# Moving work across the entrance to the second attention of a gated cross-attention and mixture-of-experts kernel

## The reference

```
x = x + tanh(g_xattn[0]) * L0_xattn(layernorm(x), ctx)    # projections, stablemax attention
x = x + tanh(g_ffn[0])   * L0_ffn(layernorm(x))           # 64 experts, top 8, capacity 128, and a shared expert
x = x + tanh(g_xattn[1]) * L1_xattn(layernorm(x), ctx)    # softmax(q k^T) v per head, q = layernorm(x), k = v = ctx
x = x + tanh(g_ffn[1])   * L1_ffn(layernorm(x))           # 256->1024, butterfly, gelu, butterfly, 1024->256
```

## Time and profile before

| | |
|---|---|
| median of 3 runs | 1233.26 us (1229.75 to 1236.8) |
| profiled execution, own time | 1231.84 us |
| its span | 1229.6 us |
| PE busy | 1034.0 us, 84% |
| DVE busy | 817.2 us, 66% |
| ACT busy | 702.2 us, 57% |
| POOL busy | 360.6 us, 29% |
| mean granted TensorE clock | 0.927 |

### The profile page before, as it was taken

One profiled execution on the slowest core, in us unless ns is written; L12 is line 12 of the kernel. 1 busy time (PEld: TensorE's weight loads), 2 busy tenths in 40 slices (PEclk: granted clock), 3 DMA queues, 4 the chain that ended last, 5 costly groups with the idle time before them and its releaser, 6 DMA issues.

```text
span 1229.6 us, 17473 instructions
## 1 busy us (share of the span) xinstructions
PE 1034.0 (84%) x5635; PEld 751.7 (61%) x5635; DVE 817.2 (66%) x2051; ACT 702.2 (57%) x1351; POOL 360.6 (29%) x313
## 2 busy tenths in 40 slices
PE   4688888888876688998899976888898989899888
PEld 2354544544444577887687755657676767767567
DVE  4468778777778766755667658687567577664543
ACT  1899878988975433565554421364455455544542
POOL 2000000000000003778777631124334251423223
PEclk9779988988887888999999996899999999999998
DMA  6564435434121323788988644331312133120000
GB/s 145 122 153 137 129 95 167 120 82 129 52 73 69 128 61 104 184 203 199 245 198 184 146 119 92 88 109 26 106 46 80 37 104 82 50 56 1 20 18 18
DMA packets 97401, 128.41 MB, mean 104 GB/s; under 512 B 26976, under 2 KB 69344, under 8 KB 97056
## 3 DMA queue, kind: packets, MB, share of 16 engines
q1 hardware_dynamic: 82448, 105.73, 30.0%
q0 software_dynamic: 12288, 18.88, 8.5%
q10 hardware_dynamic: 2576, 2.69, 1.0%
HBM read 66.15 MB, written 30.70 MB: 79 GB/s over the span
## 4 chain that ended last, share of the span: by engine, by line
PE 51%; DVE 26%; ACT 9%; issue 6%; POOL 3%; DMA 2%; SPq 2%; ACTq 2%; DVEq 0%; POOLq 0%
PE psum L912 6%; PE psum L1098 6%; PE psum L1083 5%; PE psum L1001 4%; PE psum L928 4%; PE psum L819 3%; DVE stats L1363 3%; PE psum L795 3%; PE psum L865 3%; PE psum L1030 2%; DVE weights L1484 2%; DVE peaks L1764 2%; PE psum L960 2%; PE psum L741 2%; DVE normed L1404 2%
## 5 line engine op out<-in xcount | busy, mean ns | idle before, releaser
L1863 POOL TENSOR_SCALAR vareps<-moments 128x4 f32<-128x4 f32 x32 | 10.4, 326 | 529.2 <-DVE moments L1366 529.2
L795 PE MATMUL psum<-q_stack,k_stack 96*128 96x512 f32 (+1 forms) x256 | 123.2, 511 | 39.2 <-DVE weights L1484 24.8
L1297 ACT ACTIVATE weights<-psum 128x512 f32<-128x512 f32 x160 | 94.1, 597 | 71.7 <-PE psum L795 60.7
L1484 DVE SCALAR_TENSOR_TENSOR weights<-psum,weights 128x512 f32<-128x512 f32 x160 | 102.5, 681 | 43.2 <-ACT weights L1162 43.0
L1883 POOL DMA_INDIRECT expert_sums<-made,sum_rows x64 | 105.4, 1647 | 59.3 <-DVE made L1734 38.6
L1910 POOL TENSOR_TENSOR hidden<-hidden_whole,hidden 128x512 fp32r<-128x512 f32 x64 | 82.3, 1287 | 114.2 <-DVE hidden L1812 114.2
L1030 PE MATMUL psum<-k_stack,q_stack 96*128 96x256 f32 x256 | 88.2, 395 | 31.9 <-DVE peaks L1764 20.0
L1764 DVE TENSOR_REDUCE peaks<-psum 128x2 f32<-128x308 f32 x256 | 107.0, 469 | 12.1 <-PE psum L1032 11.6
L912 PE MATMUL psum<-feat_parts,w_shared_up 128*128 128x512 f32 x384 | 100.5, 412 | 10.7 <-DVE shared_silu L1608 6.3
L1098 PE MATMUL psum<-w_con_high,hidden 128*128 128x256 f32 x512 | 102.2, 298 | 0.1
L1812 DVE CAST hidden<-hidden_whole 128x512 fp32r<-128x512 f32 x64 | 52.7, 823 | 71.6 <-ACT hidden_whole L1326 70.3
(11 more groups left out here) (211 smaller groups left out, 2390.9 us busy)
## 6 DMA issues: line engine op xcount, KB each, us to landing
expert_w<-in_expert_w SPq DMA_DIRECT2D x64, 384.0 KB
q_stack<-q_stage SPq DMA_DIRECT2D x96, 128.0 KB, 3.0
q_stack<-q_stage SPq DMA_DIRECT2D x174, 64.0 KB, 2.0
expert_sums<-zeros SPq DMA_DIRECT2D x6, 1408.0 KB, 8.2
fetched<-expert_sums SPq DMA_DIRECT2D x16, 512.0 KB, 4.8
rows_scratch<-rows SPq DMA_DIRECT2D x8, 640.0 KB, 3.4
k_raw<-in_k SPq DMA_DIRECT2D x16, 300.0 KB
x<-in_x SPq DMA_DIRECT2D x8, 512.0 KB, 4.8
```

The source lines that it names most:

```text
L795: T.matmul(to, k[0:row, head_at(head), :], q[0:row, head // 2, :], start=True, stop=True).then_inc(scored, 1)
L1297: A.activation(weights1[n % 6][:, :], score_bank[n % 2], ACT.Exp).then_inc(exped, 1)
L1484: V.scalar_tensor_tensor(weights[n % 9][:, :], score_bank[n % 5], 1.0, weights[n % 9][:, :], ALU.add, ALU.max).then_inc(weighted, 1)
```

## The change

- SP no longer fetches half 0 with `fetch(0)` behind the barrier. When all scatters have landed, and before SP waits for the other engines, `fetch_first` loads half 0 of both sums as four DMAs of two tiles each, and the first two parts of the keys follow. They signal on four semaphores of `x_in` that served the first load of x.
- DVE adds half 0 in four instructions of 512 elements instead of two of 1024, and takes the statistics of two tiles behind each pair.
- POOL's `add_experts(1, ...)` waits for the four `key_split1` of DVE instead of the norm of half 0.
- The statistics, norm, `turn_q1` and all sends of half 1 move from between the maxima of half 0 to behind `peaks(0)`, around the first `sh_down`; the second `sh_down` moves from chunk 0 to in front of `scores1(0)`. All 24 sends of half 1 are SP's (six were ACT's).
- Four units of maxima of half 1 move from in front of the loop into it, the others up to two chunks later, and `peaks(1)` from chunk 10 to chunk 12.

```diff
-PEAKS_SECOND = (-1, -1, -1, -1, 1, 2, 3, 4, 5, 6, 7, 7, 8, 8, 9, 9)
+PEAKS_SECOND = (1, 2, 2, 3, 4, 4, 5, 6, 6, 7, 8, 8, 9, 10, 10, 11)
...
 def plan_last():
-    plan = [("fetch", 0), ("load_k1", 0, 0), ("load_k1", 0, 1)]
+    plan = []
...
-    beside_peaks = {4: norm_units("q1", 1)[:2], 7: norm_units("q1", 1)[2:],
-                    9: [("turn_q1", 1), ("send_q1", 1, 0), ("send_q1_a", 1, 1)]}
     for n in range(HT * PAIRS // 2):
         plan.append(("peak", 0, n % HT, n // HT))
-        plan += beside_peaks.pop(n, [])
         if n in LATE_AT:
             late.step()
-    plan.append(("peaks", 0))
-    plan += [("send_q1", 1, two) for two in range(2, PAIRS // 2)]
+    plan += [("peaks", 0)] + norm_units("q1", 1)
     late.step()
-    plan += peak_units(1, -1)
+    plan += [("turn_q1", 1)] + [("send_q1", 1, two) for two in range(PAIRS // 2)]
+    late.step()
     plan.append(("scores1", 0))
...
+        first_sums = x_in[0:2 * SUMS]
...
+            def tile_stats(n, h, t):
+                V.bn_stats(stats[n % 2][:, t, :], x[:, HT * h + t, :]).then_inc(ln_bn, 1)
+
             def norm_stats(kind, h):
                 n = norm_no[kind, h]
-                for t in range(HT):
-                    V.bn_stats(stats[n % 2][:, t, :], x[:, HT * h + t, :]).then_inc(ln_bn, 1)
+                if (kind, h) != ("q1", 0):
+                    for t in range(HT):
+                        tile_stats(n, h, t)
...
-                    else:
-                        V.wait_ge(x_first, SUMS)
...
-            def add_experts(h, i):
+            def add_experts(h, a):
                 if h == 0:
-                    V.wait_ge(fetched_in[i], 16)
-                    if i:
-                        V.wait_ge(x_first, i)
-                    V.tensor_tensor(half_of(0), half_of(0), fetched[i][:, :, :], ALU.add).then_inc(x_first, 1)
+                    tiles = slice(2 * a, 2 * a + 2)
+                    for i in range(SUMS):
+                        V.wait_ge(first_sums[SUMS * a + i], 32)
+                        if i:
+                            V.wait_ge(x_first, SUMS * a + i)
+                        V.tensor_tensor(x[:, tiles, :], x[:, tiles, :], fetched[i][:, tiles, :],
+                                        ALU.add).then_inc(x_first, 1)
+                    V.wait_ge(x_first, SUMS * (a + 1))
+                    for t in range(2 * a, 2 * a + 2):
+                        tile_stats(norm_no["q1", 0], 0, t)
...
                     elif h == 1:
-                        G.wait_ge(ln_normed, HT * (norm_no["q1", 0] + 1))
+                        G.wait_ge(keys_split, BATCH + 4)
...
+            def fetch_first():
+                for i in range(SUMS):
+                    S.wait_ge(scattered[i], 16 * (EXPERTS // SUMS))
+                for a in range(2):
+                    for i in range(SUMS):
+                        S.dma_start(fetched[i][:, 2 * a:2 * a + 2, :], sum_dram[i][2 * P * a:2 * P * (a + 1), :].rearrange(
+                            "(t p) f -> p t f", p=P)).then_inc(first_sums[SUMS * a + i], 16)
...
                 if h == 1:
-                    S.wait_ge(x_first, SUMS)
+                    S.wait_ge(x_first, 2 * SUMS)
...
                     S.drain().then_inc(stage_over, 1)
+                    if n == 2:
+                        fetch_first()
+                        load_k1(0, 0)
+                        load_k1(0, 1)
                     S.wait_ge(stage_over, 5 * n)
```

More of the change, by code:

```diff
@@ L1892, in add_experts @@
                 if h:
-                    G.wait_ge(fetched_in[i], 16 * (h + 1))
+                    G.wait_ge(fetched_in[i], 16 * h)
                     if h >= HALVES - LATE:
@@ L2026, in send_lists @@
                                 list_dram[g].rearrange("(a e) b -> e a b", a=NA)).then_inc(list_in, 16)
+            def fetch_first():
[5 more added lines that the diff above has]
+                            "(t p) f -> p t f", p=P)).then_inc(first_sums[SUMS * a + i], 16)
             def fetch(h):
                 if h == 1:
-                    S.wait_ge(x_first, SUMS)
-                elif h:
+                    S.wait_ge(x_first, 2 * SUMS)
+                else:
                     S.wait_ge(x_added, SUMS * (h - 1))
```

## The result

| | before | after |
|---|---|---|
| median of 20 runs each, compared with each other | 1231.76 us (1227.45 to 1240.68) | 1238.91 us (1231.24 to 1246.35) |
| profiled execution, own time | 1231.84 us | 1232.08 us |
| its span | 1229.6 us | 1230.3 us |
| mean granted clock, profiled execution | 0.927 | 0.929 |
| first PE work behind the barrier to the end of the span | 507.7 us | 513.4 us |

The ratio is 1.0053, with a 95% interval of 1.003 to 1.0076: the change costs about 6.5 us. The forecast was 1234.4 us.

The account below looks back on a forecast made before the run. PE paces the kernel, but half 0 hangs on how early SP sends half 2; earlier gains end in SP's 24 sends and POOL's addition, moving that send from 805.74 to 806.8, +1.1 us on 1233.26: 1234.4 us, range 1227.5 to 1239.5.

Parts of the forecast that it names:

- the upper bound of the sum: First send of half 2: at worst +5.0 us, against the forecast's +1.1.
- no gain from the first sums: Start of half 0: upper-bound case in which the early loads come no earlier, +2.3 us.
- late keys: Last key loads before the maxima of half 0: upper-bound case with keys at 739.7, +0.8 us.
- transposes at half clock: Chunk 12, before the sends of half 2: upper-bound case of slow transposes, +0.8 us.
- The steps up to the loop: Barrier to scores1(0): shorter sums and maxima, first send of half 1 at 768.4, scores1(0) 5.6 us ahead.
- The step that failed: Chunk 10: the loop, about 5.5 us ahead, leaves DVE waiting about 2 us for POOL's sum at 793.4.
- The maxima's move into the loop: Loop of half 0: taken at nothing, covered by waits of DVE and PE; 3.4 us without that cover.
- The sign by which the forecast wanted to be found wrong: Chunk 10: statistics of half 2 released by PE or DVE and not by POOL's addition.
- rival B: Chunks 18 and later: new PE waits bring a half-clock stretch of 14 us, costing 7, giving 1241 us; chance 0.10.
- The last term: Chunks 10 to 12: from x of half 2 at 793.4, statistics through maxima sends, to the first send at 806.8.
- Rival A: Loop of half 0: its 5.6 us lead survives and statistics of half 2 do not wait, 1227.7 us; chance 0.20.
- Rival C: Barrier: early loads bring nothing because barrier or traffic holds them, +1.1 + 2.3, 1236.7 us; chance 0.08.

Follow-up runs that it names:

- e4: Changed kernel plus eight unread matmuls on PE in front of the first maxima of half 1: 1229.54 us, ratio to before 0.9991.
- e8: Changed kernel with the sums of half 2 fetched and added early, plus eight unread matmuls at PE's chunk 1 wait: 1225.50 us, ratio to before 0.994.
- e3: Changed kernel with POOL's addition to half 2 held until DVE finished the maxima of chunk 7: 1232.43 us, ratio to before 1.0002.
- e6: Changed kernel with the sums of half 2 fetched and added during the maxima of half 0: 1233.74 us, ratio to before 1.0008.
- e2: Kernel before with only the moves of half 1 (norm, transposes, all sends, later maxima): 1235.66 us, ratio to before 1.0034.
- e7: Changed kernel with the second six sends of half 1 back on ACT's queue: 1233.82 us, ratio to before 1.0013.
- e12: Front-only kernel (e1) with all maxima of half 1 in the loop and both sh_down in front of it: 1231.28 us, ratio to before 0.9992.
- e1: Changed kernel with norm, transposes, sends and maxima plan of half 1 put back as before: 1227.09 us, ratio to before 0.9956.
- e9: Kernel before with only the early loads, the smaller additions and tile_stats of the change: 1227.88 us, ratio to before 0.9971.
- e10: Kernel before with only POOL's addition to half 1 waiting for the fourth key split: 1233.74 us, ratio to before 1.0001.
- e5: Front-only kernel (e1) with the sums of half 2 fetched and added long before the loop: 1223.92 us, ratio to before 0.9927.
- e11: e5 plus 18 unread matmuls on PE in front of the maxima of half 0: 1235.73 us, ratio to before 1.0002.

## Why the prediction was right in its number and wrong in its mechanism

**The number is right by luck.** 1238.91 us lies 0.6 us inside the range. The range starts from 1233.26, the median of the first three runs of before; all 20 have 1231.76. Measured against before, the loss of 6.5 us is more than the upper bound of the sum, +5.0. And of the three terms that made this bound, no gain from the first sums (+2.3), late keys (+0.8) and transposes at half clock (+0.8), only the last came. Most of the loss was made where the prediction had put nothing, in the loop between `scores1(0)` and chunk 10.

**The steps up to the loop held.** Statistics of half 0 end at B + 8.5 (forecast 2.3 us earlier than before; it was 10.7 before). L1615 0.69. The fourth L1615 3.2 us earlier (forecast 2.9). 28 reductions in 11.93 (11.95), maxima done 8.35 earlier (8.0). First send of half 1 at B + 46.5 (768.4, which is 46.5). `scores1(0)` 5.95 earlier (5.6). 24 sends in 15.37 (16.05), `fetch(2)` at B + 61.9 (62.6), POOL starts at B + 66.0 and is through at 70.9 (71.5).

**The step that failed** is the one that stands without a number of its own: "By then DVE stands at chunk 10 in front of the statistics, since the loop runs about 5.5 us ahead", and with it "The maxima's move into the loop I take at nothing". From `scores1(0)` to chunk 10 the forecast gave the loop about 21 us (770.4 to 791.4, its wait of about 2 us in front of 793.4). It took 26.2, and so DVE was the late one, not POOL (undisturbed, as in e4 and e8, the loop takes 18.5: with that, DVE would have waited even longer than forecast). The sign by which the forecast wanted to be found wrong is there: the statistics of half 2 were released by PE and the maxima.

The runs split this delay. With the meeting of POOL and L1791 taken away the loop needs 22.7 us (e3) and 22.6 (e6): 3.5. With PE's clock held as well it needs 18.5 (e4) and 18.4 (e8): 4.2 more. As the filler alone takes both away (e4), the meeting in the change is itself in part a consequence of the slow clock. The forecast had written the first off ("the old stall at chunk 7 goes, as POOL now adds later"): POOL did start later, 3.2 us counted from B, but the loop had lost its lead by then: L1791 came at B + 66.05, where it was B + 65.92 before, and they met at 782.93 and 782.97. The second it had named, a new wait of PE "at chunk 1 for the first sends of half 1", and given to rival B.

**The last term** was 1.0 us short: from the start of the statistics to send 2 it gave 13.4 us. All kernels with the maxima moved took 14.4 (14.36 to 14.44 in after, e2, e3, e4, e6, e7, e8 and e12), and in all of them the eight transposes ran at half clock, 1.97 us where e1 has 1.34; that was an upper bound of the forecast, +0.8. Where the maxima stand as before it is 8.35. So the difference is 2.9 us of later statistics (B + 74.4 instead of 71.5) plus 1.0 here: 88.8 instead of 84.9.

**Rival B was the mechanism**, with the wrong place and nearly the right price. It gave 1241 us and had the stretch fall "in chunks 18 and later"; it fell in chunks 1 to 6, and a second one, behind the meeting, was in 786.4 to 793.2. The clocks of all executions bear out that the time at half clock has the size of the loss. The mean granted clock over the 20 executions of the changed kernel is 0.920; over 108 of before, in the four groups of experiments, it is 0.926; the four slowest of the changed one (1245 to 1246 us) had 0.909 to 0.915. With only the two levels 1.0 and 0.5, a mean of 0.920 over some 1237 us is 2 x 0.080 x 1237 = 198 us at half clock, and 0.926 over 1232 us is 182; half of these 16 us is 8, against 6.5 measured. With the filler of e4 the mean is 0.930. The Trainium skill (TensorE: Matmul & The Clock Gate, "HAM oscillation — how this bites in real kernels") counts the loss in the same way, as the half-clock time multiplied by one half; the measured difference is somewhat smaller, as it would be if PE is not the bound in all of these stretches.

**Rival A** (the lead survives) did not hold for the change: of the lead of 5.95 us at `scores1(0)` nothing was left at send 2. Without the moves of half 1 most of a smaller lead survives: 2.5 of 3.3 us in e1. That e1 gained 5.4 us, near the 5.6 of rival A, is a coincidence of size. **Rival C** (early loads bring nothing) is refuted by the trace, in which the wait is gone and the statistics end 2.3 us earlier; the 0.9971 of e9 fits, but its interval doesn't shut out 1.

**What of the change costs what.** Front part -4.4 parts in a thousand (e1), of which the loads have -2.9 (e9) and POOL's later addition by itself nothing that can be told (e10). Maxima in the loop +3.6 (e1 to e12, their intervals overlap). Norm and sends of half 1 behind the maxima of half 0, all on SP: +6.1 (e12 to after); that part makes PE wait for the first six sends, and `fetch(2)`, now behind 24 sends, keeps POOL beside L1791 although the loop is later. In sum +5.3. This split holds for this order of steps only, because the two parts of the change don't add: the front part gains 4.4 (e1), the moves of half 1 without it cost 3.4 (e2), and together they cost 5.3, some 6 more than the sum. The traces of e2 and of the change show what differs: behind the same wait at chunk 1 (1.89 us in both) the clock was at half for 3.4 us in e2 and for almost 10 in the change, and only in the change did L1791 meet POOL.

**What stays open.** The executions of the changed kernel at 1240 us and more have no trace. That they hold more half-clock time is shown by their mean clock; where in the kernel it lies is not. Nor is it shown why single traced executions (e3, e9, e12) needed 430 to 436 us behind send 2 where the others needed 421 to 428. For e9 and e12 the meeting of POOL with the norm is a part of it; e3 doesn't have it. Open is also why the same wait at chunk 1 was followed by so short a stretch at half clock in e2.

## What to carry to other kernels

When work is moved so that an engine runs ahead, ask first whether TensorE keeps its clock up to the place from which the gain is counted: a new wait of under 2 us right behind a light phase cost 4 us in the loop here and led to a further stall behind it, and eight matmuls that nobody reads in its place gave back 6.2 parts in a thousand, all of the loss (e4). Bring a shared input (here POOL's sum) in so early that neither the wait for it nor a meeting with VectorE's reads of on-chip memory depends on a microsecond; with the early loads, that made the version with the lowest ratio (e5). Don't add up two parts that were measured alone: here a gain of 4.4 and a loss of 3.4 parts in a thousand made a loss of 5.3. And look at the spread of the runs: where it shrinks with the edit (from 15 us in 20 runs to 4 in 12 with the eight matmuls), that is a sign that the edit has hit a cause of it.

## What the runs showed of the hardware that was not expected

- A short wait was enough to lose the clock. In three kernels (after, e3, e6) PE waited 1.88 to 1.91 us for the first sends, behind a little work (1.20 us in the three from 765 in after), and then had a granted clock of 0.50 for about 10 us, though it worked without a gap in most of it. In e2 the same wait of 1.89 us was followed by 3.4 us at 0.50. Eight matmuls of 2.00 us in that wait kept it at 1.00 (e4, e8). Put into a phase that is light anyway, 18 of them did not keep it (e11: 0.50 again by 750), and the kernel was 9 us slower.
- A two-source addition on POOL holds up DVE beyond the three-operand instruction: `SCALAR_TENSOR_TENSOR` 0.48 to 2.5 and 2.6 us (e1, after), four `TENSOR_SCALAR` from and to on-chip memory 1.38 to 3.49 and 5.50 us (e12, e9). Reductions that read PSUM took 0.41 us each beside it (six in 2.44 at 785.48, while POOL added until 787.77). The Trainium skill (SBUF — State Buffer, "SBUF: two separate sides") describes an exclusive lock held for a whole instruction; the trace agrees: L1791 started 0.04 us behind POOL's first addition (half of 4.84 us) and took 2.59 us.
- ACT pays for sends in its own work: six of them, with a table load of 1.28 us behind them, kept `exp1(0)` back until 770.67, and PE for 3.41 us (e7).
